# Scan kernel on one core: B tables loaded for eight steps at a time, gate loads in 256 KB pieces, next layer's weights later

## The chip, the cores and the metric

One core of a Trainium2 chip runs the whole program. The metric is the device time in microseconds (us) of one execution; the time before is the median of three runs. The engines are TensorE (PE; PEld are its weight loads), VectorE (DVE), ScalarE (ACT), GpSimd (POOL) and SyncE (SP), which here computes nothing and issues nearly all DMA transfers, one after the other ("SPq" in the rows).

## What is computed

Four residual layers on x of shape (64 sequences, 64 positions, 256 channels): two of attention, then two of a selective state space model. The change lies in the last two. Cut to what matters, for D_INNER = 512 and D_STATE = 16:

```python
xr, gate = split(x @ W_in.T); xc = silu(conv(xr + t_emb)); xn = layernorm(xc)
Bm, Cm, dt = split(xn @ W_xproj.T, 3)
Ad = 1.0 + tanh(dt @ W_dt.T + b_dt) * 0.01 * A
Bd = Bm * minimum(norm(xn), 1.0)
def step(h, inputs):                       # h: (64 sequences, 16, 512)
    ad, bd, xt, ct = inputs
    h = clip(h * ad[:, :, None] + bd[:, :, None] * xt[:, None, :], -10.0, 10.0)
    return h, einsum('bd,bdh->bh', ct, h)
y = scan(step) + D * xn                    # 64 positions, one after the other
x = x + (y * silu(gate)) @ W_out.T
```

## The kernel before

The 64 sequences are 8 groups of 8 (G = 8). Each of the two scan layers (l = 0, 1) has a front part (projections, convolution, norm, per group), a scan, and a post part (gate and output projection, per group). The scan works on four groups at once (QW = 4), so a layer has two passes of 64 steps (PASSES = 2). The state q is 128 partitions (8 sequences by 16 states) by 4 by 512, float32.

A step is a loop over three engines. PE forms the outer products B x in PSUM (`inputs`, line 1520: five matmuls with 96 rows of contraction). ACT (line 1068) and POOL (line 626) multiply the old state by the decay into R. DVE adds R to PSUM and clips in three custom instructions (line 2064). PE then forms y from the new state (`y_of`, line 1533), ACT copies it out every four steps. PSUM is not doubled for the inputs: `inputs` of step n starts when DVE has finished the first instruction of step n-1, and no earlier.

The 96 rows are 3 parts of x (bfloat16 pieces of a float32 number) by 8 sequences by 4, where the fourth is a row of zeros; B has 3 such parts as well. Partition 4r+i holds x row r and B part i. The x rows and the B tables come from DRAM, where the front part has put them (`xpart_d`, `bdiag_d`), two steps a load: `load_x(ps, k)` brings steps 2k and 2k+1 into slot k % 4 of both `Uw` (B) and `xq` (x), in three transfers of 48 KB for B (24 rows of 2 KB, line 411) and three of 192 KB for x (24 rows of 8 KB, line 415). All six raise the same semaphore `xq_in[k % 4]`, on which PE waits before an even step. The zero rows of `Uw` are set once by a memset on POOL (line 577).

SP's program is written out by hand. In each pass there are eight rounds `c2` of eight steps; a round has four turns `s8`. Each turn waits until PE has done the inputs of step 8 c2 + 2 s8 + 1 (`x_done_with`, semaphore `pe_w`), which frees one slot, and then loads steps 6 to 7 further on (`load_x(ps, 4*c2 + s8 + 4)`). Behind certain turns other work is queued, in program order:

- `store_y` in turns 0 and 2: y of four steps, 256 KB;
- in pass 0: `store_parts` (three transfers of 512 KB), `store_decay`, `store_b` (six small ones) and `store_x` of the last two groups, and in round 6 `load_tables(1)` (eight transfers of 32 KB);
- in pass 1: `load_gate(0)` behind round 1 and `load_gate(1)` behind round 2 (each two transfers of 1 MB: `xnp` and `sgp`), `load_front(1)` behind round 3 (the next layer's weights, six transfers, some 1.3 MB, layer 0 only), `load_y(0)` and `load_y(1)` behind round 4 (four transfers of 512 KB), `load_y(2)` and `load_y(3)` in round 7.

The end of a scan starts the post part, which needs the gates (semaphores `po_in`), y and Wo.

Of the kernel before, what the change touches and what calls it, by code (L numbers as in the profile page):

```python
# [10 lines left out]
P = 128  # L11
GB = P // N
# [20 lines left out]
ROW = QW * GB * N  # L33
DIAG = PARTS * S * ROW
SSM_LOADS = 6
# [8 lines left out]
def cond_resid_kernel(nc, xT, condT, attw, win, wconv, chan, wxp, wdt, dtv, wout, dskip,  # L44
# [19 lines left out]
    with es:  # L64
# [77 lines left out]

        Uw = sb("Uw", [P, XB, XT, QW, GB, N], bf16, where=ssm)
        sb("By", [P, 2, CH, QW, STRIP], bf16, where=ssm)
# [107 lines left out]
        pad_r = sem("pads_set")  # L252
        one_in = [sem("still_rows0"), sem("still_rows1")]
        zero_r, zero_in = sem("zeros_set"), sem("diagonal_zeroed")
        bt_mm, pd_r = sem("bturn_mm"), sem("decayed_odd_ready")
# [19 lines left out]
        PICK = 4 * 16  # L275
        XQ = 2 * PARTS * 16
        PW = QW + 1
# [35 lines left out]
        def _(sp):  # L313
# [25 lines left out]
            sp.wait_ge(x_done, LAYERS * G + 1)  # L339
            sp.wait_ge(set_r, 2)  # L340
            for l in range(LAYERS):
# [23 lines left out]
                def store_b(it, ps, w):  # L365
                    sp.wait_ge(tv_s, it * 4 + 4 + TV0)
                    alone(sp)
                    for b in range(2):
                        rows = bdiag_d[ps].rearrange("(j b r) -> j b r", b=2, r=DIAG + N)[:, b, 0:DIAG]
                        rows = rows.rearrange("j (i t w c n) -> i w c t j n", i=PARTS, t=S, w=QW, c=GB)  # L370
                        for i in range(PARTS):
                            sp.dma_start(rows[i, ds(w, 1), 0].rearrange("a t j n -> (a t) j n"),
                                         tvp[b * S:(b + 1) * S, i, :].rearrange("p (j r) -> p j r", r=LANE)[:, :, 0:N]).then_inc(tv_st, 16)
# [22 lines left out]
                def load_tables(ps):  # L396
                    Cc, At = pass_tables[ps]
                    q0 = ps * QW
                    for dst, src in ((Cc, cc_d), (At, a_d)):
                        for g in range(QW):  # L400
                            sp.dma_start(dst[:, g, :], src[q0 + g, :, 0:N, :]).then_inc(tab_in[ps], 16)

                def still_rows(b):
                    half_x = xq[:, b * (XB // 2):(b + 1) * (XB // 2), :, :, :].rearrange("p k g t c -> p (k g t c)")
                    for i in range(PARTS, SPREAD):
                        sp.dma_start(half_x[i:XROWS:SPREAD, :], still_d).then_inc(one_in[b], 16)

                def load_x(ps, k):
                    rows = bdiag_d[ps, 0:GB * DIAG].rearrange("(b i f) -> i b f", i=PARTS, f=S * ROW)
                    for i in range(PARTS):  # L410
                        sp.dma_start(Uw[i:XROWS:SPREAD, k % XB, :, :, :, :].rearrange("p t w b n -> p (t w b n)"),
                                     rows[i, :, k * (XT * ROW):(k + 1) * (XT * ROW)].unsqueeze(0)
                                     .broadcast_to([PARTS, GB, XT * ROW])).then_inc(xq_in[k % XB], 16)
                    for i in range(PARTS):
                        sp.dma_start(xq[i:XROWS:SPREAD, k % XB, :, :, :].rearrange("p t g c -> p (t g c)"),
                                     xpart_d[ps, :, :, k * XT:(k + 1) * XT, :, :].rearrange("j b t g c -> (j b) (t g c)")).then_inc(xq_in[k % XB], 16)
# [5 lines left out]
                def load_y(g):  # L422
                    for b2 in range(2):
                        sp.dma_start(y_tile(g)[b2 * S:(b2 + 1) * S, :, :],
                                     y_d[:, g].rearrange("k (t j b) c -> b k t j c", t=CH, b=2)[b2]).then_inc(yl_in[g % YB], 16)

                def load_gate(g):
# [27 lines left out]
                for k in range(XB // 2):  # L455
                    load_x(0, k)
                store_decay(l * G + G - 2, G - 2)
                sp.wait_ge(zc_r, l * (G * DC) + G * DC)
# [6 lines left out]
                for ps in range(PASSES):  # L465
# [5 lines left out]
                    for c2 in range(CHUNKS // 2):  # L471
                        for s8 in range(4):
# [3 lines left out]
                            if c2 + 1 < CHUNKS // 2:  # L476
                                load_x(ps, 4 * c2 + s8 + XB)
                            elif ps + 1 < PASSES:
                                load_x(ps + 1, s8)
                            elif s8 < 2:  # L480
                                alone(sp)
                                load_y(2 + s8)
                            if s8 == 0 and (c2 or ps):
                                store_y(ps - (c2 == 0), (2 * c2 - 1) % CHUNKS)
                            if s8 == 2:
                                store_y(ps, 2 * c2)
                            if ps == 0 and (c2, s8) == (0, 1):
                                store_parts(l * G + G - 2, 1, QW - 2)
# [15 lines left out]
                        if ps + 1 == PASSES and c2 == 0:  # L504
                            sp.wait_ge(sg_st, l * (16 * G) + 16 * G + 16)
                            sp.wait_ge(xf_st, l * (16 * G) + 16 * G + 16)
                            alone(sp)
                        if ps + 1 == PASSES and c2 in (1, 2):
                            load_gate(c2 - 1)
                        if ps + 1 == PASSES and c2 == 3 and l + 1 < LAYERS:  # L510
                            load_front(l + 1)
# [26 lines left out]
        def _(pl):  # L538
# [37 lines left out]
            pl.memset(Wy[:, :, :, :], 0.0).then_inc(set_r, 1)  # L576
            pl.memset(words(Uw), 0.0).then_inc(set_r, 1)
            pl.wait_ge(set_r, 2)
            alone(pl)
# [507 lines left out]
        def _(pe):  # L1087
# [253 lines left out]
            for l in range(LAYERS):  # L1341
# [168 lines left out]
                alone(pe)  # L1510
                def inputs(pi, c2, s8, first=False):
                    n = c2 * 8 + s8
                    hb = s8 // XT % XB
                    if s8 % XT == 0:
                        pe.wait_ge(xq_in[hb], (pi * (HALVES // XB) + c2 + s8 // 8) * XQ + XQ)
                    if first and s8 in (0, 4):
                        pe.wait_ge(one_in[s8 // 4], (l + 1) * (16 * (SPREAD - PARTS)))
                    for w, begin, end, bank, unit in ((0, 0, DI, 0, 1), (1, 0, DI // 2, 1, 1), (1, DI // 2, DI, 2, 2), (2, 0, DI, 3, 2), (3, 0, DI, 5, 3)):
                        pe.wait_ge(dv_q, pi * (UN * S) + n * UN + unit)
                        pe.matmul(PS[:, bank, begin:end], Uw[0:XROWS, hb, s8 % XT, w, :, :].rearrange("p b n -> p (b n)"),  # L1520
                                  xq[0:XROWS, hb, s8 % XT, w, begin:end], start=True, stop=True).then_inc(pe_w, 1)
# [14 lines left out]

                inputs(l * PASSES, 0, 0, True)
                for ps in range(PASSES):
                    pi = l * PASSES + ps
                    plain = TAIL if ps == 0 else 1  # L1540
                    for c2 in range(plain):
                        for s8 in range(8):
                            if ps == 0:
                                last_group(c2 * 8 + s8)
                            inputs(pi, c2, s8 + 1, ps == 0 and c2 == 0)
                            y_of(pi, c2, s8)
                    with pe.Fori(plain, CHUNKS // 2 - 1) as c2:
                        for s8 in range(8):
                            inputs(pi, c2, s8 + 1)
                            y_of(pi, c2, s8)  # L1550
                    for s8 in range(8):
# [39 lines left out]
        def _(v):  # L1591
# [292 lines left out]
            for l in range(LAYERS):  # L1884
# [196 lines left out]
                def gated(g):  # L2081
                    it, u = l * G + g, g % 2
                    v.wait_ge(po_in[u], (l * (G // 2) + g // 2) * 32 + 32)
                    if it:
# [88 lines left out]
```

## Time and profile before

| what | value |
|---|---|
| runs | 1834.01 us median of 3 (1826.44 to 1843.92) |
| the profiled execution | 1831.48 us, of which the span of the records is 1829.7 us |
| PE / DVE / ACT / POOL busy | 90% / 85% / 66% / 32% of the span |
| scan of layer 0 | 743.7 to 1107.7 us |
| scan of layer 1 | 1385.5 to 1745.5 us |
| DMA queue of SP | 242.57 MB, 40.6% of 16 DMA engines' span |
| xq loads, Uw loads | 384 of 192 KB, 384 of 48 KB |

Times in the profile are counted from the start of the span. A group row gives busy time and the idle time just before it with what ended it. For SP a row is the time in which it issues transfers; when they land is not in it. With two busy engines coupled by a step, the question for the scan is not who is busiest but what DVE, the engine that carries the state, waits for.

### The profile page before, as it was taken

To read this page: it belongs to the slowest core of one execution; us is meant where nothing else is said; L and a number is where in the kernel's file an instruction comes from. 1 tells how busy PE (TensorE), PEld (TensorE's weight loads), DVE (VectorE), ACT (ScalarE), POOL (GpSimd) and SP (SyncE) were. 2 spreads that over 40 slices of the span, in tenths; PEclk is the share of its full clock that TensorE was granted. 3 is DMA by queue.
4 is the path that set the end of the run, shared out by engine and by line. 5 is a ranking of instruction groups with operands and counts; after the bars stand their busy time and mean duration, and the time that the engine had idled before them with its cause. 6 is when DMAs were issued, how large, how long until landed. Compare 5 with 4: busy or idle time off the path is not lost. (4 is left out here: it accounts for less than half of the span.)

```text
span 1829.7 us, 42381 instructions
## 1 busy us (share of the span) xinstructions
PE 1640.9 (90%) x14036; PEld 714.1 (39%) x14036; DVE 1561.6 (85%) x2132; ACT 1212.6 (66%) x2017; POOL 586.8 (32%) x822
## 2 busy tenths in 40 slices
PE   7999999999999999788797879999997887978898
PEld 3555555555554555222121214445552221211144
DVE  5899999999887999889797877679998997978865
ACT  5646555555647999788777771079997887878710
POOL 0223232322321112455454540011224554545400
PEclk9999999999999999899898989999998998999899
DMA  4000003000002454555556667524545555566687
GB/s 159 2 1 0 1 2 108 2 1 0 1 1 93 160 171 169 158 176 187 160 181 227 213 203 243 177 84 168 171 163 161 180 187 162 179 219 210 197 238 261
DMA packets 123040, 245.87 MB, mean 134 GB/s; under 512 B 50000, under 2 KB 75856, under 8 KB 104912
## 3 DMA queue, kind: packets, MB, share of 16 engines
q1 hardware_dynamic: 122496, 242.57, 40.6%
q10 hardware_dynamic: 432, 1.84, 0.3%
q8 instruction: 67, 1.10, 0.2%
q14 instruction: 45, 0.37, 0.1%
HBM read 158.25 MB, written 86.11 MB: 134 GB/s over the span
## 5 line engine op out<-in xcount | busy, mean ns | idle before, releaser
L2064 DVE CUSTOM_DVE_ANT_0 q<-R,PS 128x768 f32<-128x768 f32 x756 | 597.9, 857 | 99.1 <-PE PS L1520 87.3
L1068 ACT ACTIVATE R<-q,Ast 128x512 f32<-128x512 f32 x756 | 508.9, 715 | 123.2 <-DVE q L2064 82.5
L1520 PE MATMUL PS<-xq,Uw 96*128 96x512 bf16 (+1 forms) x1280 | 342.1, 360 | 110.7 <-DMA xq<-xpart_d 65.9
L626 POOL TENSOR_TENSOR R<-q,Ast 128x256 f32<-128x256 f32 x504 | 308.5, 612 | 362.1 <-DVE q L2064 307.4
L1533 PE MATMUL PS<-q,Wy 128*32 128x512 f32 x2048 | 289.7, 632 | 3.4 <-ACT ys L1055 2.7
L1520 PEld LDWEIGHTS PS<-xq,Uw 96*128 96x128 bf16 x1280 | 93.7, 100 | 479.4 <-DVE q L2064 348.7
L1189 PE MATMUL PS<-X,Win 128*128 (+1 forms) x456 | 213.7, 606 | 0.1
L1090 PE MATMUL PS<-xn,Wl 128*128 128x512 f32 x384 | 188.0, 614 | 0.7 <-DVE xn L1646 0.7
L1764 DVE SCALAR_TENSOR_TENSOR acc<-xp,Wc,acc 128x512 f32<-128x512 f32 x192 | 134.5, 748 | 2.6
L557 POOL TENSOR_TENSOR ex<-ex,rs 128x1024 f32<-128x1024 f32 x32 | 76.8, 2400 | 164.2 <-DVE rs L1669 164.2
L1189 PEld LDWEIGHTS PS<-X,Win 128*128 128x128 f32 x456 | 82.5, 191 | 92.4 <-issue 91.6
L1573 PE MATMUL PS<-yg,Wo 128*128 128x512 f32 x256 | 113.5, 597 | 0.0
L550 POOL TENSOR_TENSOR vsc<-vTd,vs_t 128x1024 f32<-128x1024 f32 x16 | 41.6, 2602 | 216.1 <-ACT vTd L767 216.1
L791 ACT ACTIVATE acc<-xp,Ch,Wc 128x512 f32<-128x512 f32 x64 | 51.9, 815 | 76.0 <-DVE xp L1760 75.8
L775 ACT ACTIVATE pT<-PS 128x512 f32<-128x512 f32 x128 | 69.3, 594 | 41.9 <-PE PS L1167 41.9
L767 ACT ACTIVATE vTd<-PS 128x1024 f32<-128x1024 f32 x32 | 32.8, 1024 | 86.4 <-PE PS L1090 86.4
L1090 PEld LDWEIGHTS PS<-xn,Wl 128*128 128x128 f32 x384 | 66.2, 191 | 56.2 <-issue 51.8
L1656 DVE TENSOR_REDUCE mx<-PS 128x32 f32<-128x2048 f32 x32 | 73.1, 2284 | 15.1 <-PE PS L1151 14.9
L2088 DVE SCALAR_TENSOR_TENSOR yf<-xnp,Dsk,PS 128x512 f32<-128x512 f32 x64 | 43.5, 742 | 44.6 <-DMA sgp<-sg_d 38.3
L1666 DVE TENSOR_REDUCE sm<-ex 128x32 f32<-128x2048 f32 x32 | 73.0, 2281 | 7.7 <-ACT ex L779 7.7
L1167 PE MATMUL PS<-ident,ex 128*128 128x128 f32 x512 | 69.3, 277 | 7.6 <-DVE ex L1673 5.7
L1533 PEld LDWEIGHTS PS<-q,Wy 128*32 128x32 f32 x2048 | 43.9, 110 | 81.5 <-issue 73.7
(160 smaller groups left out, 2438.2 us busy)
## 6 DMA issues: line engine op xcount, KB each, us to landing
xq<-xpart_d SPq DMA_DIRECT2D x384, 192.0 KB
Uw<-bdiag_d SPq DMA_DIRECT2D x384, 48.0 KB
sg_d<-sg SPq DMA_DIRECT2D x16, 1024.0 KB, 5.5
xn_d<-z SPq DMA_DIRECT2D x16, 1024.0 KB, 4.0
y_d<-ys SPq DMA_DIRECT2D x64, 256.0 KB, 4.3
xnp<-xn_d SPq DMA_DIRECT2D x16, 1024.0 KB, 9.1
sgp<-sg_d SPq DMA_DIRECT2D x16, 1024.0 KB, 13.5
xpart_d<-xh SPq DMA_DIRECT2D x16, 512.0 KB, 3.0
```

The source lines that it names most:

```text
L557: pl.tensor_tensor(late_half(ex, r), late_half(ex, r), rs[:, r, :].rearrange("p (j e) -> p j e", j=4)[:, :, 4:8] .unsqueeze(3).broadcast_t ...
L626: pl.tensor_tensor(R[:, 1, cols], q[:, (t + 1) % 2, 1, cols], Ast[:, h, 1, t:t + 1].broadcast_to([P, DI // 2]), ALU.mult).then_inc(pd_r, 1)
L1068: act.activation(R[:, w, :], q[:, (t + 1) % 2, w, :], ACT.Copy, scale=Ast[:, h, w, t:t + 1]).then_inc(ac_r, 1)
L1090: mm = pe.matmul(PS[:, bank, :], Wl[l][:, w, c, m * P:(m + 1) * P], rhs[:, c, :], start=(c == 0), stop=(c == HC - 1))
L1189: mm = pe.matmul(PS[:, m % DC, :], Win[:, c, m * P:(m + 1) * P], X[:, ds(g, 1), c, :].rearrange("p a t -> p (a t)"), start=(c == 0), stop= ...
L1520: pe.matmul(PS[:, bank, begin:end], Uw[0:XROWS, hb, s8 % XT, w, :, :].rearrange("p b n -> p (b n)"), xq[0:XROWS, hb, s8 % XT, w, begin:end ...
L1533: mm = pe.matmul(PS[32 * w:32 * w + 32, 4, :], Wy[:, h, w, t * 32:(t + 1) * 32], q[:, s8 % 2, w, :], start=(t == 0), stop=(t == CH - 1), s ...
L1573: mm = pe.matmul(PS[:, 4 + 2 * (g % 2) + m, :], Wo[:, c, m * P:(m + 1) * P], yg[:, g % 2, c, :], start=(c == 0), stop=(c == DC - 1))
L1656: v.tensor_reduce(mx[:, r, :], PS[:, 0:4, :].rearrange("p j (e k) -> p (j e) k", k=S), AX.X, ALU.max).then_inc(max_r, 1)
L1666: v.tensor_reduce(sm[:, r, :], ex[:, r, :, :].rearrange("p j (e k) -> p (j e) k", k=S), AX.X, ALU.add).then_inc(sum_r, 1)
L1764: v.scalar_tensor_tensor(out=tiled(acc[:, m, :]), in0=xp[:, m, :, j:j + S], scalar=Wc[:, m, j:j + 1], in1=tiled(acc[:, m, :]), op0=ALU.mul ...
L2064: v._custom_dve(bass.dve_ops.TENSOR_ADD_SAT, out=state, in0=R[:, :, :].rearrange("p w c -> p (w c)")[:, begin:end], in1=fed, s0=CLIP, s1=- ...
```

## The change

- The B tables get a layout in DRAM with four parts instead of three, the fourth zero (`DIAG` grows by a third, and the zeroing of `bdiag_d` during attention from 12 to 16 transfers of 256 KB), so that 32 rows of eight steps (8 KB each) are one transfer.
- `Uw` holds two buffers of eight steps. `load_b(ps, c2)` fills one in three transfers of 256 KB, on a semaphore of its own (`u_in`). PE waits for it before the first step of each round. In a round it is issued once, in turn 3, for the round after the next.
- `load_x` issues only its three x transfers; `XQ` halves.
- At the start of the scan the order on SP is x for steps 0 to 3, then B of rounds 0 and 1, and later x for steps 4 to 7.
- `load_gate(0)` and `load_gate(1)` are split: `load_piece` brings 256 KB of `xnp` and 256 KB of `sgp` behind each x load of rounds 1 and 2 of the last pass. The later gates are loaded as before.
- `load_front(l + 1)` moves from behind round 3 to behind round 5.
- The memset of `Uw` on POOL goes, and with it one count of `set_r`.
- PE's loop over rounds has 16 steps in its body instead of 8, since the buffer of B alternates.

```diff
-DIAG = PARTS * S * ROW
+DIAG = 4 * S * ROW
+UB = 2 * 4
-        Uw = sb("Uw", [P, XB, XT, QW, GB, N], bf16, where=ssm)
+        Uw = sb("Uw", [P, 2, UB, QW, GB, N], bf16, where=ssm)
-        XQ = 2 * PARTS * 16
+        XQ = PARTS * 16
+                def load_b(ps, c2):
+                    rows = bdiag_d[ps, 0:GB * DIAG].rearrange("(r f) -> r f", f=S * ROW)
+                    for j in range(PARTS):
+                        sp.dma_start(Uw[SPREAD * GB * j:SPREAD * GB * (j + 1), c2 % 2, :, :, :, :].rearrange("p t w b n -> p (t w b n)"),
+                                     rows[:, c2 * (UB * ROW):(c2 + 1) * (UB * ROW)]).then_inc(u_in[c2 % 2], 16)
+
                 def load_x(ps, k):
-                    rows = bdiag_d[ps, 0:GB * DIAG].rearrange("(b i f) -> i b f", i=PARTS, f=S * ROW)
-                    for i in range(PARTS):
-                        sp.dma_start(Uw[i:XROWS:SPREAD, k % XB, :, :, :, :].rearrange("p t w b n -> p (t w b n)"),
-                                     rows[i, :, k * (XT * ROW):(k + 1) * (XT * ROW)].unsqueeze(0)
-                                     .broadcast_to([PARTS, GB, XT * ROW])).then_inc(xq_in[k % XB], 16)
+                def load_piece(g, m):
+                    for dst, src in ((xnp, xn_d), (sgp, sg_d)):
+                        sp.dma_start(dst[:, g % 2, m, :], src[g, :, m, :]).then_inc(po_in[g % 2], 16)
                 for k in range(XB // 2):
                     load_x(0, k)
+                load_b(0, 0)
+                load_b(0, 1)
+                            if s8 == 3 and (c2 + 2 < CHUNKS // 2 or ps + 1 < PASSES):
+                                load_b((ps + (c2 + 2) // (CHUNKS // 2)), (c2 + 2) % (CHUNKS // 2))
+                            if ps + 1 == PASSES and c2 in (1, 2):
+                                load_piece(c2 - 1, s8)
-                        if ps + 1 == PASSES and c2 in (1, 2):
-                            load_gate(c2 - 1)
-                        if ps + 1 == PASSES and c2 == 3 and l + 1 < LAYERS:
+                        if ps + 1 == PASSES and c2 == 5 and l + 1 < LAYERS:
                             load_front(l + 1)
-            pl.memset(words(Uw), 0.0).then_inc(set_r, 1)
-                def inputs(pi, c2, s8, first=False):
+                def inputs(pi, k, s8, c=None, first=False):
+                    c2 = k if c is None else c * 2 + k
+                    u, twos = (k + s8 // 8) % 2, (k + s8 // 8) // 2 + (0 if c is None else c)
+                    if s8 % 8 == 0:
+                        pe.wait_ge(u_in[u], (twos + pi * (CHUNKS // 4)) * (PARTS * 16) + PARTS * 16)
-                    with pe.Fori(plain, CHUNKS // 2 - 1) as c2:
-                        for s8 in range(8):
-                            inputs(pi, c2, s8 + 1)
-                            y_of(pi, c2, s8)
+                    with pe.Fori(0, (CHUNKS // 2 - 1 - plain) // 2) as c:
+                        for k in (plain, plain + 1):
+                            for s8 in range(8):
+                                inputs(pi, k, s8 + 1, c)
+                                y_of(pi, c * 2 + k, s8)
```

SP at the start of a scan, before. The rows name destination and source of the transfers, their shape and their number; `still_d` is zeros, `cc_d` and `a_d` are stores of group 6, `tvp` its B.

```order
L406 DMA xq<-still_d 24x8192
L411 DMA Uw<-bdiag_d 24x1x1024 x3
L415 DMA xq<-xpart_d 24x4096 x3
L411 DMA Uw<-bdiag_d 24x1x1024 x3
L415 DMA xq<-xpart_d 24x4096 x3
L356 DMA cc_d<-Cn 4x32x64 x2
L356 DMA a_d<-am 4x32x64 x2
L406 DMA xq<-still_d 24x8192
```

The same place in the changed kernel:

```order
L407 DMA xq<-still_d 24x8192
L417 DMA xq<-xpart_d 24x4096 x6
L412 DMA Uw<-bdiag_d 32x4096 x6
L358 DMA cc_d<-Cn 4x32x64 x2
L358 DMA a_d<-am 4x32x64 x2
L407 DMA xq<-still_d 24x8192
```

Step 0 now needs B of round 0, which is issued behind x of steps 0 to 3; the number of transfers ahead of the stores stays twelve.

SP in the second pass of layer 0, before: turns 2 and 3 of round 1, the first gate loads, turn 0 of round 2.

```order
L411 DMA Uw<-bdiag_d 24x1x1024 x3
L415 DMA xq<-xpart_d 24x4096 x3
L420 DMA y_d<-ys 128x512
L411 DMA Uw<-bdiag_d 24x1x1024 x3
L415 DMA xq<-xpart_d 24x4096 x3
L428 DMA xnp<-xn_d 128x2048
L429 DMA sgp<-sg_d 128x2048
L411 DMA Uw<-bdiag_d 24x1x1024 x3
L415 DMA xq<-xpart_d 24x4096 x3
L420 DMA y_d<-ys 128x512
```

The same turns in the changed kernel:

```order
L417 DMA xq<-xpart_d 24x4096 x3
L422 DMA y_d<-ys 128x512
L431 DMA xnp<-xn_d 128x512
L431 DMA sgp<-sg_d 128x512
L417 DMA xq<-xpart_d 24x4096 x3
L412 DMA Uw<-bdiag_d 32x4096 x3
L431 DMA xnp<-xn_d 128x512
L431 DMA sgp<-sg_d 128x512
L417 DMA xq<-xpart_d 24x4096 x3
L422 DMA y_d<-ys 128x512
```

The six transfers of a turn have become three, the B load comes once a round, and the gates come in two quarter-size transfers a turn instead of two whole ones between two turns.

## Rows read from the trace of the kernel before

**Rows 1.** Waits of DVE, whole program: engine, line, awaited, us in total, times, longest.

```profile
DVE q L2064 <- PE PS L1520: 87.3, 47, 7.9
DVE q L2064 <- ACT R L1068: 6.4, 10, 1.2
```

**Rows 2.** Waits of PE, whole program, same columns.

```profile
PE PS L1520 <- DMA xq<-xpart_d: 65.9, 25, 7.8
```

**Rows 3.** Windows: the four passes; length, busy us, PE clock, DMA share, GB/s.

```profile
743.70:930.90 187.20, 156.88 (x977) 40.76 (x975) 160.97 (x217) 144.44 (x228) 90.00 (x165) 0.93 0.54 174
930.90:1107.70 176.80, 149.55 (x833) 33.77 (x832) 151.18 (x193) 135.39 (x205) 84.61 (x155) 0.92 0.66 208
1385.50:1570.00 184.50, 154.85 (x977) 40.38 (x975) 160.97 (x216) 144.48 (x228) 89.98 (x165) 0.94 0.54 175
1570.00:1745.50 175.50, 148.65 (x834) 33.26 (x832) 151.24 (x193) 135.48 (x205) 84.69 (x155) 0.94 0.65 204
```

**Rows 4.** Timeline of DVE, layer 0: start, length, instructions, idle before and releaser.

```profile
875.10 2.42 DVE L2064 CUSTOM_DVE_ANT_0 q<-R,PS 128x768 f32<-128x768 f32 x3 [4.32 <-PE PS L1520]
...
996.27 2.42 DVE L2064 CUSTOM_DVE_ANT_0 q<-R,PS 128x768 f32<-128x768 f32 x3 [6.89 <-PE PS L1520]
...
1019.62 2.42 DVE L2064 CUSTOM_DVE_ANT_0 q<-R,PS 128x768 f32<-128x768 f32 x3 [2.84 <-PE PS L1520]
...
1041.13 14.20 DVE L2064 CUSTOM_DVE_ANT_0 q<-R,PS 128x768 f32<-128x768 f32 x18 [0.72 <-PE PS L1520]
...
1068.52 2.42 DVE L2064 CUSTOM_DVE_ANT_0 q<-R,PS 128x768 f32<-128x768 f32 x3 [7.91 <-PE PS L1520]
1072.21 35.53 DVE L2064 CUSTOM_DVE_ANT_0 q<-R,PS 128x768 f32<-128x768 f32 x45 [1.27 <-PE PS L1520]
```

**Rows 5.** Timeline of SP, second pass, round 0: start and length of the issuing.

```profile
940.43 2.24 SPq L411 DMA_DIRECT2D Uw<-bdiag_d  x3
942.72 2.30 SPq L415 DMA_DIRECT2D xq<-xpart_d  x3
945.06 0.52 SPq L420 DMA_DIRECT2D y_d<-ys  x1
```

**Rows 6.** Waits of SP in the window 743.7 to 930.9.

```profile
SPq L411 <- PE PS L1520: 10.4, 19, 1.2
```

**Rows 7.** Timeline of SP and PE around the first load_y of layer 0.

```profile
1048.19 1.28 SPq L424 DMA_DIRECT2D y_space<-y_d  x2
1049.52 1.26 SPq L424 DMA_DIRECT2D spare_y<-y_d  x2
1050.82 2.32 SPq L411 DMA_DIRECT2D Uw<-bdiag_d  x3
1053.19 2.30 SPq L415 DMA_DIRECT2D xq<-xpart_d  x3
...
1067.52 1.88 PE L1520 MATMUL PS<-xq,Uw 96*128 96x512 bf16 x5 [7.78 <-DMA xq<-xpart_d]
```

**Rows 8.** Windows of 2 us in pass 1; last three columns clock, DMA share, GB/s.

```profile
984.00:986.00 2.00, 2.00 (x14) 0.60 (x15) 1.36 (x2) 0.97 (x2) 0.25 (x2) 1.00 1.00 360
990.00:992.00 2.00, 0.00 (x0) 0.00 (x0) 0.00 (x0) 0.15 (x1) 0.00 (x0) 0.72 0.73 232
1056.00:1058.00 2.00, 1.91 (x14) 0.38 (x12) 2.00 (x3) 1.09 (x3) 0.74 (x2) 1.00 1.07 218
```

**Rows 9.** Timeline of SP and PE at the first step of layer 0.

```profile
736.02 2.31 SPq L415 DMA_DIRECT2D xq<-xpart_d  x3
...
742.83 2.45 PE L1520 MATMUL PS<-xq,Uw 96*128 96x512 bf16 x6
```

**Rows 10.** Timeline of DVE: waits for PE where no load is late.

```profile
769.95 2.41 DVE L2064 CUSTOM_DVE_ANT_0 q<-R,PS 128x768 f32<-128x768 f32 x3 [0.46 <-PE PS L1520]
...
933.78 6.47 DVE L2064 CUSTOM_DVE_ANT_0 q<-R,PS 128x768 f32<-128x768 f32 x8 [0.49 <-PE PS L1520]
...
1454.31 2.42 DVE L2064 CUSTOM_DVE_ANT_0 q<-R,PS 128x768 f32<-128x768 f32 x3 [0.62 <-PE PS L1520]
```

## What the change should do to the time

> **What bounds the kernel now.** I read the waits of DVE first, since DVE carries the state through the scan. It waited 87.3 us for PE's inputs, 47 times, and only 6.4 us for ACT [rows 1]. PE's own waits name the cause: 65.9 us, 25 times, for the load of x [rows 2]; 87.3 is more because PE restarts slowly behind each such wait. The windows of the four passes give the frame: 724.0 us in all, DVE busy 160.97 + 151.18 + 160.97 + 151.24 = 624.4, so 99.6 us idle [rows 3]. The timeline of DVE says where: a run of 45 instructions, 15 steps, takes 35.53 us, 2.37 us a step, without a gap; the big gaps are single, 4.32 us in pass 0 and 6.89, 2.84, 0.72 and 7.91 us in pass 1, each followed by one of some 1.2 us [rows 4].
>
> Why is x late? The timeline of SP shows 2.24 us to issue three B transfers and 2.30 us for three x transfers, 0.76 us each, and 0.52 us for a y store [rows 5]. With the 0.05 us between groups a turn costs 4.63 us, a store 0.57, and a round of eight steps 4 x 4.63 + 2 x 0.57 = 19.7 us. DVE needs 8 x 2.37 = 19.0 us for it. SP is slower than DVE before anything else is queued on it: in 187 us of pass 0 it waited 10.4 us for PE to free slots [rows 6]. Whatever stands in front of a load (parts, tables, gates, front weights, y) then makes SP late, and the lateness is never won back until DVE stalls.
>
> The worst case in full: step 39 began at 1026.21 + 5 x 2.37 = 1038.1 us and step 41 at 1041.13 + 2.37 = 1043.5 [rows 4], which frees the slot of step 48. SP issued that load from 1050.8 on, 7.3 us late, behind y loads issued from 1048.19; it landed at 1067.52, where PE had waited 7.78 us [rows 7].
>
> **The change part by part.** *B tables.* Per round 12 transfers of 0.75 us become three. Their issue is not in the trace; the nearest rows are the x transfers with rows of 8 KB too, 0.77 us [rows 5], and I take that: a round costs SP 12 x 0.77 + 3 x 0.77 + 2 x 0.57 = 12.7 us of 19.0. From below nothing bounds it but zero; from above, 1.5 us a transfer would still give 14.9. SP then waits for PE at each turn, and a load has its full lead: from the end of the inputs of step 2k+1, which is the start of that step on DVE, to the inputs of step 2k+8, six steps and 0.9 us later, 15.1 us. An x load alone needs 2.3 us to issue and little more to land: at the first step its last issue began near 737.6 and PE used it at 742.83 without waiting, so 5.3 us at most [rows 9]. Slack 15.1 - 2.3 - 5.3 = 7.5 us or more, where there was none. The other work on SP's queue is three to eight transfers in a round, at 0.77 us each no more than 6.2 us, and a round leaves 19.0 - 12.7 = 6.3.
>
> What this can take back is the DVE waits that a load causes. I subtract from 87.3 us those that stay: ten gaps behind PE's work for the last group, the first 0.46 and the last 0.62, 6.1 us together, and 0.49 us at step 1 of each second pass [rows 10], in all 7.1. **Removable: 80.2 us.**
>
> *Gates in pieces.* 8 turns of a layer carry 512 KB more. The full rate was 360 GB/s with the 1 MB transfers under way, 232 where x loads were left alone, and 218 with rows of 2 KB, as the pieces have [rows 8]. A turn then moves 576 KB of x (2.5 us), 192 KB of B at 360 (0.5), 512 KB of gates at 218 (2.3) and 128 KB of y at 218 (0.6): 5.95 us against 4.74. If nothing overlaps, 8 x 1.21 = 9.7 us pile up against a slack of 7.5: at most 2.2 us a layer. If x and gates overlap, as the 360 GB/s suggest, nothing. I take 0. SP's own time for the pieces, 8 x 0.64 as for the y loads [rows 7] = 5.1 us a round, brings a round to 17.8 us, below 19.0.
>
> *The first load_y* is not split, so it is the one burst left. Before, 19.3 us passed from its first issue to the landing of the load behind it [rows 7]. Now it is issued when step 39 has begun, behind x (2.3) and B (2.3), at +5 us, and the load behind it is needed at step 48's inputs, +19.9. With the old 19.3 us it lands at +24.3, a stall of 4.4 us and 1.3 behind it; with bytes alone (0.77 of B, 2.1 of y, 0.58 of x, 0.26 stored, at 360 to 218 GB/s, 10.3 to 17 us) it lands at +15.3 to +22. Range 0 to 5.7 us a layer; I take 2.0, nearer to the bytes, since the old case had two B sets and a second x load in flight: **-4.0 us**.
>
> For those bytes the Trainium skill has a rule, page "DMA: Bandwidth & Descriptors", section "Why a DMA increments its semaphore by 16 and not by 1": a transfer runs on the largest number of engines up to 16 that divides the slowest dimension of both sides. By it the old B transfers (a broadcast dimension of 3) ran on 3 engines, x (24 rows) on 12, and the new B (32 rows) on 16; the trace agrees as far as the DMA share of 0.73 with only x and B loads left goes [rows 8], and no row shows single engines. By an estimate from that page the most loaded engines then carry 60 KB a turn instead of 96, and the term here would be 0 and not 4: 1753 us.
>
> *The start.* B of round 0 is the third group issued, its last issue one group of 2.3 us later than that of x for step 0 was, so it lands 0 to 2.3 us after PE asks at 742.83 [rows 9]. I take 1.0 a layer: **-2.0 us**.
>
> *At nothing:* four more zeroing transfers and the memset lie in attention, where SP idles; the front weights now follow round 5 with 15 steps of the pass left, and the post part of layer 0 needs them last; B's loads have a lead of over eight steps. PE's loop executes the same matmuls per step in a longer body; before, the 15 steps at 2.37 us ran out of the loop into straight code without a gap [rows 4]. DVE, ACT and POOL keep their work; the idle ACT waits I leave in.
>
> **Sum.** 80.2 - 4.0 - 2.0 = 74.2 us off the profiled execution's 1831.48: 1757 us. The median of the runs, 1834.01, lies 2.5 us above it, inside their spread of 17, and I add nothing.
>
> **Rivals.**
> *A. The bursts cost, not SP's lateness.* For it: 7.3 us of lateness stand beside 19.3 us of transfer [rows 7], and the pieces bring the same bytes with shorter rows. Against: SP issued without a pause where no burst was near [rows 5], and the 4.32 us of pass 0 [rows 4] fell behind a smaller burst, the 1.5 MB of the part stores. Then the y stall stays whole, 9.2 us in layer 0 and about as much in layer 1, and half of the others, 5.5, 8.2 and 4.1 us with their second gaps: 18.4 + 17.8 = 36 us remain, 1831.5 - 80.2 + 36 = **1788 us**, with the start's 2 us well inside the roundness of this.
>
> *B. The change does not do what it says: issuing is not the limit.* The Trainium skill says on the same page, "Issuing engines are not separate DMA queues", that the time to initiate is "usually small relative to the DMA itself". As a mechanism of this kernel: x moves 576 KB a turn at 232 GB/s, 2.5 us, plus y and B; were that what fills the 4.7 us of a turn, only the B bytes would matter, and they grow by a third. Then the stalls stay but for 10 us at the gates: **1822 us**. Against it: 4.54 us of issuing in a turn of 4.74 [rows 5], which is not small; the page's sentence would leave this rival the likeliest.
>
> *C. Slower: B late each round.* PE now waits for B before 28 rounds whose B is loaded during the scan. If B came late, all of those would stop. Break-even is 74.2 / 28 = 2.7 us each; 1% slower, 92 / 28 = 3.3 us: **1850 us**. B's issue ends 5 us after step 8c+7 begins and is needed 9 x 2.37 - 1.5 = 19.8 us after it, 14.8 us later; to be 3.3 late it would need 18 us from its last issue. Behind the y burst a load took 12.8 us at worst [rows 7]. Little speaks for it.
>
> **How the numbers follow.** The forecast 0.73, its own range 1746 to 1771: all 80.2 and a part of ACT's 6.4 gone below; y stall in full, gates 2.2 and start 2.3 in each layer above (7.4 + 4.4 + 2.6 = 14 us). A 0.16, B 0.05, C 0.03, and 0.03 for better than 1746. The range to be held 8 times in 10 reaches from 1744 to 1788: it takes in the forecast and the better half of A. About 1% is what a measurement of this kernel can tell from no change, so faster means below 1816: the forecast, A and the better case, 0.92; same 0.05; slower 0.03.
>
> **What would show it.** Right: DVE's wait for PE falls from 87.3 to some 13 us; PE's wait for x nearly goes; SP waits for PE some 6 us in a plain round; steps 24, 32 and 44 without a gap; a gap of 0 to 5.7 us at step 48. Wrong: gaps before steps 33 to 40 (gate pieces), waits for Uw at multiples of eight (C), or SP still issuing without a pause (B transfers dearer than 0.77 us). If DVE's instructions or ACT's get longer with more DMA traffic beside them, the floor of 2.37 us a step falls as a basis.

## Result: 1770 us, 3.3% faster

| | us | runs |
|---|---|---|
| before | 1831.35 median (1826.44 to 1843.92) | 4 |
| changed kernel | 1770.45 median (1761.81 to 1774.35) | 4 |
| ratio | 0.9665, 95% interval 0.9629 to 0.9701 | |
| changed kernel, profiled execution | 1761.81, span 1760.0 | |
| forecast | 1757, range 1744 to 1788 | |

Waits in the changed kernel, whole program: engine, line, awaited, us in total, times, longest. Lines 2078 and 2075 are DVE's steps (2075 is the first of a pass), 1533 PE's inputs, 417 the x loads on SP.

```profile
DVE q L2078 <- PE PS L1533: 13.0, 16, 1.7
DVE q L2075 <- PE PS L1533: 12.8, 2, 6.7
DVE q L2078 <- ACT R L1077: 7.5, 8, 1.2
PE PS L1533 <- DMA Uw<-bdiag_d: 10.3, 2, 5.4
PE PS L1533 <- DMA xq<-xpart_d: 8.0, 7, 2.0
SPq L417 <- PE PS L1533: 177.5, 109, 3.7
```

DVE's wait for PE in the steps fell from 87.3 to 13.0 us [rows 1], PE's wait for x from 65.9 to 8.0 us [rows 2]. SP waits 177.5 us for free slots. In the kernel before it was a quarter of that:

```profile
SPq L411 <- PE PS L1520: 43.6, 70, 2.4
```

A wait that was not there has appeared: 10.3 us for `Uw`, twice, before the first step of each scan.

The four passes as windows, with the columns of [rows 3]:

```profile
748.30:916.40 168.10, 153.91 (x978) 38.00 (x975) 160.23 (x217) 144.54 (x228) 89.90 (x165) 0.97 0.70 206
916.40:1071.30 154.90, 143.90 (x835) 31.76 (x834) 150.43 (x193) 135.27 (x205) 84.51 (x155) 1.00 0.87 236
1351.80:1520.80 169.00, 155.31 (x977) 38.26 (x975) 160.22 (x216) 144.52 (x228) 89.91 (x165) 0.96 0.70 204
1520.80:1676.30 155.50, 143.97 (x835) 31.87 (x836) 150.62 (x193) 135.40 (x205) 84.58 (x155) 1.00 0.84 227
```

Together 647.5 us against 724.0, DVE busy 621.5 of them (624.4 before), so 26.0 us idle against 99.6. DVE works as long as before and waits less. The granted clock of PE in the second pass is 1.00 in both layers, instead of 0.92 and 0.94. Before, it was down to 0.72 in a stretch in which PE stood idle [rows 8]; idle times of 7 us are gone from that pass. The start of the two scans gave back 12.8 - 2.4 = 10.4 us of DVE's waits (2.4 is what DVE waited there before); PE waited 5.4 and 4.9 us for B. The windows begin behind those waits and so do not hold them. The passes gave 724.0 - 647.5 = 76.5 us, the starts took 10.4: 66.1 of the 69.7 us by which the span is shorter are thereby found. The other 3.6 are spread over the parts outside the scans.

SP in the second pass of the changed kernel, start and length of the issuing:

```profile
933.82 2.27 SPq L417 DMA_DIRECT2D xq<-xpart_d  x3
936.13 1.44 SPq L412 DMA_DIRECT2D Uw<-bdiag_d  x3
938.47 2.29 SPq L417 DMA_DIRECT2D xq<-xpart_d  x3
940.80 0.51 SPq L422 DMA_DIRECT2D y_d<-ys  x1
```

An x transfer costs SP 0.76 us as before [rows 5], a B transfer with 32 rows only 0.48. Between them SP pauses.

### The profile page after: what moved, and what is told of

Read it like the earlier page. It is cut to its first block and busy times, and to the rows that moved or that the text cites. A ratio compares the mean times of both kernels' runs of the same rounds, so it can differ in the third digit from the quotient of the medians.

```text
span 1760.0 us, 42112 instructions
## 1 busy us (share of the span) xinstructions
PE 1627.5 (92%) x14036; PEld 705.4 (40%) x14036; DVE 1559.0 (89%) x2132; ACT 1212.5 (69%) x2017; POOL 584.7 (33%) x821
## 3 DMA queue, kind: packets, MB, share of 16 engines
q10 hardware_dynamic: 432, 1.84, 0.3%
## 5 line engine op out<-in xcount | busy, mean ns | idle before, releaser
L1546 PE MATMUL PS<-q,Wy 128*32 128x512 f32 x2048 | 280.9, 613 | 2.6 <-ACT ys L1064 1.9
L1533 PEld LDWEIGHTS PS<-xq,Uw 96*128 96x128 bf16 x1280 | 85.7, 97 | 437.7 <-DVE q L2078 374.6
L2102 DVE SCALAR_TENSOR_TENSOR yf<-xnp,Dsk,PS 128x512 f32<-128x512 f32 x64 | 43.6, 743 | 42.3 <-DMA sgp<-sg_d 36.0
L611 POOL CAST middle<-remain 128x128 bf16<-128x128 f32 x14 | 4.1, 293 | 218.7 <-DVE remain L1912 218.7
```

The lines of the kernel that those rows point to most:

```text
L1533: pe.matmul(PS[:, bank, begin:end], Uw[0:XROWS, u, s8 % 8, w, :, :].rearrange("p b n -> p (b n)"), xq[0:XROWS, hb, s8 % XT, w, begin:end], ...
L1546: mm = pe.matmul(PS[32 * w:32 * w + 32, 4, :], Wy[:, h, w, t * 32:(t + 1) * 32], q[:, s8 % 2, w, :], start=(t == 0), stop=(t == CH - 1), s ...
```

## Experiments

Each ran beside the kernel before on its chip; ratios are to that. Edits are shown against the changed kernel where nothing else is said; arrays, counts and waits that only follow from them are left out. The theories: SP's issuing is too slow for DVE (*lateness*); the few DMA engines on which B and x run are the limit (*few engines*); the large transfers hold the loads up (*bursts*).

### B alone

```diff
-                            if ps + 1 == PASSES and c2 in (1, 2):
-                                load_piece(c2 - 1, s8)
+                        if ps + 1 == PASSES and c2 in (1, 2):
+                            load_gate(c2 - 1)
-                        if ps + 1 == PASSES and c2 == 5 and l + 1 < LAYERS:
+                        if ps + 1 == PASSES and c2 == 3 and l + 1 < LAYERS:
```

> The changed kernel with only the B tables changed: the first gates come in whole transfers of 1 MB behind rounds 1 and 2, and the front weights behind round 3, as before the change. Theory of SP's lateness: a load has 15 us of lead, so the bursts are mostly hidden; 0 to 4 us of stalls a layer, 1770 to 1778 us. Theory of the bursts: the stalls at steps 24 and 32 of the second passes come back, 8.4 + 4.3 us in each layer: about 1795 us.

Measured: 1766.85 us (1761.01 to 1774.52), ratio 0.9675 (0.9630 to 0.9721). The B tables bring the whole gain. Timeline of DVE in the second pass of layer 0 of this kernel:

```profile
917.92 111.15 DVE L2078 CUSTOM_DVE_ANT_0 q<-R,PS 128x768 f32<-128x768 f32 x141 [0.49 <-PE PS L1533]
1037.91 2.42 DVE L2078 CUSTOM_DVE_ANT_0 q<-R,PS 128x768 f32<-128x768 f32 x3 [8.84 <-PE PS L1533]
1041.59 35.47 DVE L2078 CUSTOM_DVE_ANT_0 q<-R,PS 128x768 f32<-128x768 f32 x45 [1.27 <-PE PS L1533]
```

141 instructions, steps 1 to 47, run without one gap past the whole gate loads and the front weights; at step 48, behind the y loads, 8.84 us remain. So the bursts theory falls for the gates; behind y a stall is left in this layer. Here the front weights had gone by shortly before y. In layer 1, which loads none, the gap at step 48 was 0.45 us.

### The gates in pieces, alone

```diff
-                        if ps + 1 == PASSES and c2 in (1, 2):
-                            load_gate(c2 - 1)
+                            if ps + 1 == PASSES and c2 in (1, 2):
+                                load_piece(c2 - 1, s8)
```

This is the kernel before with these lines (and DVE's counts for `po_in`).

> The kernel before with only the first two gates loaded in pieces of 256 KB behind the x loads. Theory of SP's lateness and of the few engines alike: neither is relieved, SP gets 12 more transfers to issue in these two rounds, the stalls move but stay: 1820 to 1838 us. Theory of the bursts: the stalls at steps 24 and 32 go, some 12 us a layer: about 1805 us.

Measured: 1826.47 us (1823.61 to 1835.75), ratio 0.9999 (0.9975 to 1.0023). No effect. DVE waited 86.0 us for PE, in 54 places instead of 47: the stalls were only shared out.

### SP kept busy

```diff
+                            if c2 + 1 < CHUNKS // 2 or ps + 1 < PASSES:
+                                for n in range(2 if s8 == 0 else 3):
+                                    sp.dma_start(idle_d[(pi * 4 * (CHUNKS // 2) + 4 * c2 + s8) * 3 + n], still_d[:, 0:32]).then_inc(idle_in, 16)
```

> The changed kernel with 11 tiny copies a round added on SP's queue (24 rows of 64 bytes from the array of zeros into unused DRAM): by 0.77 us each, 8.5 us of issuing, so that a round costs SP about 19.8 us again, as before the change, with no bytes to speak of. Theory of SP's lateness: the stalls come back, 1815 to 1835 us. Theory that the transfers' own load on few DMA engines was the limit: 1770 to 1778 us.

Measured: 1836.27 us (1834.35 to 1846.11), ratio 1.0048 (1.0029 to 1.0067). Its waits:

```profile
DVE q L2084 <- PE PS L1539: 89.2, 49, 10.8
PE PS L1539 <- DMA xq<-xpart_d: 72.3, 26, 10.7
SPq L419 <- PE PS L1539: 46.8, 70, 1.5
```

The copies carry 1.5 KB each. Issuing alone takes the whole gain back, and the waits look like those before the change: 89.2 for 87.3 us [rows 1], 72.3 for 65.9 [rows 2], and 46.8 us of SP for free slots where the kernel before had 43.6. The transfers themselves were not slower: from the first to the last event that a load of x raised on its semaphore passed 4.5 us in the median, 5.6 in the changed kernel. SP's lateness is shown as a cause.

### Three DMA engines kept busy

```diff
+                            if c2 + 1 < CHUNKS // 2 or ps + 1 < PASSES:
+                                sp.dma_start(idle_d[pi * 4 * (CHUNKS // 2) + 4 * c2 + s8, :, 0:GB * 3072].rearrange("j (b c) -> j b c", b=GB),
+                                             still_d[:, 0:3072].rearrange("(j b) c -> j b c", b=GB)).then_inc(idle_in, 16)
```

> The changed kernel with one copy a turn added, 3 by 8 rows of 6 KB (144 KB, as many bytes as the old B loads of a turn) from the array of zeros into unused DRAM, its slowest dimension 3. SP: 4 x 0.77 = 3.1 us more a round, 14.7 of 19.0 us. Theory of SP's lateness: 1765 to 1780 us. Theory of the few engines (if such a copy runs on 3 of 16, these carry 108 KB a turn, above the 96 of the kernel before): stalls of x come back, 1820 us or more.

Measured: 1859.01 us (1856.53 to 1862.20), ratio 1.0161 (1.0130 to 1.0193), with SP waiting 123.5 us for free slots. Slower than the kernel before. Two questions follow: was it the bytes as such or their spread, and would less have done?

The same 144 KB as 16 rows of 9 KB:

```diff
-                                sp.dma_start(idle_d[pi * 4 * (CHUNKS // 2) + 4 * c2 + s8, :, 0:GB * 3072].rearrange("j (b c) -> j b c", b=GB),
-                                             still_d[:, 0:3072].rearrange("(j b) c -> j b c", b=GB)).then_inc(idle_in, 16)
+                                sp.dma_start(idle_d[pi * 4 * (CHUNKS // 2) + 4 * c2 + s8, :, 0:4608], still_d[0:16, 0:4608]).then_inc(idle_in, 16)
```

> The changed kernel with one copy a turn of 144 KB as 16 rows of 9 KB, from and to the same arrays as in the run with 3 by 8 rows of 6 KB (1859 us). If the number of engines made that run slow, this one, 9 KB an engine, stays within 1% of the changed kernel: 1765 to 1782 us. If the bytes, the array of zeros or the writes to DRAM made it slow, 1840 us or more.

Measured: 1773.85 us (1768.58 to 1780.35), ratio 0.9690 (0.9665 to 0.9715), within the interval of the changed kernel's. And 3 by 8 rows of 4.5 KB, 108 KB, with which three engines would carry 96 KB a turn, as much as in the kernel before:

```diff
-                                sp.dma_start(idle_d[pi * 4 * (CHUNKS // 2) + 4 * c2 + s8, :, 0:GB * 3072].rearrange("j (b c) -> j b c", b=GB),
-                                             still_d[:, 0:3072].rearrange("(j b) c -> j b c", b=GB)).then_inc(idle_in, 16)
+                                sp.dma_start(idle_d[pi * 4 * (CHUNKS // 2) + 4 * c2 + s8, :, 0:GB * 2304].rearrange("j (b c) -> j b c", b=GB),
+                                             still_d[:, 0:2304].rearrange("(j b) c -> j b c", b=GB)).then_inc(idle_in, 16)
```

> The changed kernel with one copy a turn of 3 by 8 rows of 4.5 KB (108 KB) from the array of zeros into unused DRAM. If it runs on 3 DMA engines, these carry 60 + 36 = 96 KB a turn, as much as in the kernel before, while SP has 11.6 + 2.8 = 14.4 of 19.0 us a round to issue. Theory that the few engines were a limit of their own in the kernel before: 1815 to 1845 us, PE waiting for x while SP waits for PE. Theory that only SP's issuing was the limit at that load, and the 108 KB of the earlier run went too far: 1770 to 1785 us.

Measured: 1818.97 us (1811.97 to 1822.73), ratio 0.9930 (0.9904 to 0.9955). Its waits:

```profile
DVE q L2084 <- PE PS L1539: 68.3, 41, 9.1
PE PS L1539 <- DMA xq<-xpart_d: 54.0, 21, 9.0
SPq L419 <- PE PS L1539: 117.7, 92, 5.8
```

SP waits 117.7 us for free slots, so it is not late, and yet PE waits 54.0 us for x. With 108 KB and a slowest dimension of 3 the time is within 0.7% of the kernel before; with 144 KB in 16 it is that of the changed kernel. The shape of a transfer decides, not its bytes.

By the Trainium skill, page "DMA: Bandwidth & Descriptors", section "Why a DMA increments its semaphore by 16 and not by 1", a transfer runs on the largest number of engines up to 16 that divides the slowest dimension of both sides. The traces agree in the number of events with which a transfer raises its semaphore by 16: 4 for a copy of 3 by 8 rows and for an old B transfer, 13 for x, 16 for a new B transfer and for the copy of 16 rows. That is 3, 12 and 16, and one event more where there are fewer than 16. (The two old transfers are counted together: a load of B and x has 51 events, 3 by 4 and 3 by 13.)

The times of these events show where PE's wait comes from. A load of x has 39 of them: three that come while SP issues, and twelve for each of the three transfers as they land. Take the load that SP began to issue at 942.88 us in the run with 3 by 8 rows of 4.5 KB. Its first 30 events, 27 of them landings, had come by 948.89. Then there was none until 956.51, and the last came at 958.68. Nine is three for each transfer. From the 30th event to the last passed 5.4 us in the median of the 128 loads; in the changed kernel it was 1.1 us, with the 16 rows 1.0, with SP kept busy 0.4. An event does not name its engine; that the nine are those of the three engines with the copy on them is inferred from their number.

How much of this was in the kernel before? Of the 51 events there, the last 18 are all that three engines would raise for B and x together. From the 33rd to the last passed 1.8 us in the median, so these copies weighed more than the old B loads did. Of PE's 65.9 us of waiting for x, at most 39.7 fell behind the 33rd event. In the run with the copies 47.8 of 54.0 fell behind the 30th, and with SP kept busy, where B has its new shape, 21.4 of 72.3. At the worst stall before, step 48 [rows 7], the 33rd event came at 1063.40 and the last at 1067.38: 4.0 of the 7.8 us.

So either limit alone can cost this scan 49 to 66 us (1819 and 1836 against 1770). The issuing brought back alone gives the time of the kernel before, 1836 against 1831, with the new B transfers in place: by these runs their shape without the smaller number of issues would have brought nothing. What the old shape alone would have cost was not run; by the events it is less than the 49 us of the copies.

### The start of the scan

```diff
+                load_b(0, 0)
                 for k in range(XB // 2):
                     load_x(0, k)
-                load_b(0, 0)
-                load_b(0, 1)
...
                 for k in range(XB // 2, XB):
                     load_x(0, k)
+                load_b(0, 1)
```

> The changed kernel with one order altered at the start of each scan: B of round 0 is issued ahead of x of steps 0 to 3, and B of round 1 behind x of steps 4 to 7. Changed kernel: PE waits 5.4 us a layer for the first B. If B was late because of its place in the queue, PE's wait before the first step falls to 0 to 2 us in each layer and the time by 8 to 11 us, to about 1761. If the start is short of transfer rate (zero rows, x and B together), x becomes the late one instead and at most 3 us are gained.

Measured: 1760.53 us (1746.76 to 1764.46), ratio 0.9602 (0.9553 to 0.9652). DVE's wait before its first steps fell from 12.8 to 5.4 us, of which 2.4 are PE's own time: 3.0 are left of 10.4. The interval of the ratio overlaps that of the changed kernel, 0.9629 to 0.9701, so the gain is read from the waits. (The waits with B first that the next expectation quotes, 0.6 to 1.5 us, were set down too low: they were 1.0 and 2.0.) Is it the place behind x, or B of round 1 beside it?

```diff
                 load_b(0, 0)
-                load_b(0, 1)
...
                     load_x(0, k)
+                load_b(0, 1)
```

> The changed kernel with B of round 1 issued behind x of steps 4 to 7, B of round 0 left behind x of steps 0 to 3; one look, for PE's wait before the first step (5.4 and 4.9 us in the two layers of the changed kernel, 0.6 to 1.5 with B of round 0 first). If the place of B of round 0 behind x makes it late, the wait stays at 4 us or more. If the 768 KB of B of round 1, which are under way beside it, make it late, the wait falls below 2.5 us.

Measured once: 1774.89 us. PE waited 10.3 us for `Uw` in the two layers, 5.58 in layer 0: as in the changed kernel. The place behind x makes B late. That execution had a stall of 8.45 us at step 48 of the second pass, though its program is the changed kernel's there. The profile of the changed kernel shows 1.41. Why that load was late here is open.

### The y loads in halves

```diff
-                            load_y(0)
-                            load_y(1)
+                            if ps + 1 == PASSES and c2 == 5:
+                                load_y_half(s8 // 2, s8 % 2)
-                        if ps + 1 == PASSES and c2 == 5 and l + 1 < LAYERS:
+                        if ps + 1 == PASSES and c2 == 6 and l + 1 < LAYERS:
```

with B first as above.

> The changed kernel with B of round 0 first at the start, the first two y loads in four halves of 512 KB, one behind each turn of round 5 and not together behind round 4, and the front weights behind round 6. The gaps of 1 to 2 us in the second half of pass 1 go (some 3 us a layer) and so do the 3.7 us a layer of the start: 1755 us, 8 to 14 below the changed kernel. If the gaps come from the total rate (the DMA share was 0.91 there), they only move, and the time is that of the kernel with B first, 1760 us.

Measured: 1754.62 us (1751.01 to 1763.78), ratio 0.9611 (0.9577 to 0.9646), against 0.9602 with B first alone: too close to tell by the ratios. By the profile the second pass of layer 0 ran without a gap, while in layer 1 steps 30 to 33 still had gaps of 1.23, 3.54 and 1.26 us. There stand the gate pieces.

### The gate pieces on trial

Three kernels side by side on one chip. The changed kernel again:

> The changed kernel once more, beside the two below on one chip. 1762 to 1774 us as before; the spread should come from the stall at step 48 of the second pass of layer 0 (1.4 us in its first profile, 8.5 us in the run with B of round 1 later, which is alike there).

Measured: 1770.20 us (1764.98 to 1772.42), ratio 0.9672 (0.9647 to 0.9697). DVE in the second pass of layer 0, steps 24, 26, 32, 48 and 56:

```profile
973.22 4.74 DVE L2078 CUSTOM_DVE_ANT_0 q<-R,PS 128x768 f32<-128x768 f32 x6 [0.40 <-PE PS L1533]
981.10 2.42 DVE L2078 CUSTOM_DVE_ANT_0 q<-R,PS 128x768 f32<-128x768 f32 x3 [3.14 <-PE PS L1533]
...
999.91 2.42 DVE L2078 CUSTOM_DVE_ANT_0 q<-R,PS 128x768 f32<-128x768 f32 x3 [2.78 <-PE PS L1533]
...
1040.08 18.85 DVE L2078 CUSTOM_DVE_ANT_0 q<-R,PS 128x768 f32<-128x768 f32 x24 [1.48 <-PE PS L1533]
1061.49 2.42 DVE L2078 CUSTOM_DVE_ANT_0 q<-R,PS 128x768 f32<-128x768 f32 x3 [2.55 <-PE PS L1533]
```

In this execution DVE waited 27.5 us for PE in the steps, not 13.0. The first profile was of the fastest of its four runs, 1761.81; this one is of the slowest of its six, 1772.42. My guess that step 48 makes the spread did not hold here (1.48 us); the gaps at 26 and 32 do it, and one of 3.47 us at step 30 in layer 1.

The changed kernel with whole gates (`load_gate` behind rounds 1 and 2, as in the diff of B alone, front weights behind round 5):

> The changed kernel with the first two gates in whole transfers behind rounds 1 and 2. If the pieces help, the stalls at steps 24 and 32 come back, some 5 us or more: 1775 us. If a lead of 15 us hides the whole gates as well, there is no difference beyond the noise; if the pieces are what makes the gaps of 1 to 3 us at steps 30 to 32, it is 1 to 5 us faster: 1765 to 1770.

Measured: 1758.05 us (1754.24 to 1764.07), ratio 0.9612 (0.9585 to 0.9638), 12 us below the changed kernel with intervals that don't meet, and more than the 1 to 5 us expected. Its second passes:

```profile
922.13 111.13 DVE L2078 CUSTOM_DVE_ANT_0 q<-R,PS 128x768 f32<-128x768 f32 x141 [0.49 <-PE PS L1533]
1034.32 18.85 DVE L2078 CUSTOM_DVE_ANT_0 q<-R,PS 128x768 f32<-128x768 f32 x24 [1.06 <-PE PS L1533]
...
1525.70 111.16 DVE L2078 CUSTOM_DVE_ANT_0 q<-R,PS 128x768 f32<-128x768 f32 x141 [0.49 <-PE PS L1533]
```

Steps 1 to 47 in one piece in both layers. And the two findings together, with the y halves and the front weights behind round 6:

> B of round 0 first, whole gates, the first two y loads in halves over round 5, front weights behind round 6. If the pieces of the gates cost 2 to 5 us, this is the fastest version: 1748 to 1753 us. If not, it is as fast as the version with pieces, 1755 us.

Measured: **1746.57 us** (1744.57 to 1749.42), ratio 0.9551 (0.9527 to 0.9574): 24 us below the changed kernel and the fastest version of the study. Its second passes, whole:

```profile
917.71 148.99 DVE L2082 CUSTOM_DVE_ANT_0 q<-R,PS 128x768 f32<-128x768 f32 x189 [0.49 <-PE PS L1537]
...
1512.80 149.03 DVE L2082 CUSTOM_DVE_ANT_0 q<-R,PS 128x768 f32<-128x768 f32 x189 [0.49 <-PE PS L1537]
```

63 steps in 149.0 us, 2.365 us each, no gap. DVE is the bound of these passes now.

What the pieces do to the transfers can be read from one window of each kernel, at the same place in the turns of the gates of layer 0, 46.4 us behind the start of the pass (last columns DMA share and GB/s). First the changed kernel again, then the first profile of the changed kernel, then whole gates:

```profile
962.00:982.00 20.00, 15.91 (x95) 3.82 (x91) 16.40 (x22) 14.96 (x23) 9.58 (x18) 0.94 0.98 232
```

```profile
962.80:982.80 20.00, 19.20 (x116) 4.19 (x108) 19.87 (x26) 18.12 (x28) 11.53 (x22) 1.00 0.99 271
```

```profile
965.60:985.60 20.00, 19.21 (x116) 4.24 (x108) 19.87 (x26) 18.13 (x28) 11.49 (x22) 1.00 0.94 273
```

With pieces the DMA engines are full, and what they move differs from one execution to the next, 232 and 271 GB/s; with whole gates they move 273 and are busy 0.94 of the time. So the pieces leave no room, though in a good execution they move as much. The shorter rows, 2 KB instead of 8, would fit that. But the pieces also stand behind eight x loads instead of two, and the two were not separated.

## Why the prediction was right, and where it was not

- **What bounds it: right, and half of it.** SP's lateness was read from rows and the run with SP kept busy shows it. The second limit I let move only one term, by 4 us. Copies of that shape cost 49 us, and of PE's 65.9 us of waiting in the kernel before up to 39.7 may be its part. The rows showed a sign of it: the load behind the y burst landed 19.3 us after the burst began [rows 7], while the bytes alone account for 10 to 17, and I put the difference down to loads in flight. 4.0 us of it passed behind the 33rd of its 51 events.
- **80.2 us removable: right in kind.** In the steps 87.3 - 13.0 = 74.3 us went in the first profile, 87.3 - 27.5 = 59.8 in the second. My sum left 7.1 + 4.0 = 11.1 us in this row. Of the 13.0, 6.7 are the gaps behind PE's other work and at step 1 (forecast 7.1), and 6.3 are stalls by loads.
- **B at 0.77 us a transfer: too dear.** 0.48 us, so a plain round costs SP 11.7 us and not 12.7. Without effect, since SP waits anyway.
- **The start, -2.0 us: mis-sized.** It was 10.4 us. I took the landing of x at the head of the queue (5.3 us at most [rows 9]) for B, which stands behind the zero rows and two x loads. SP began to issue it at 737.46 us and PE got it at 747.49, some 8.6 us behind the last issue of that B where I had 5.3 at most. The run with B first shows the cause, the place in the queue.
- **Gates in pieces at nothing: wrong.** I bounded them at 2.2 us a layer; by the medians they cost 12 us together. The step that failed is the overlap: I took 0 because x and gates together seemed to move at 360 GB/s. A turn has 1408 KB, 1.44 MB, and the windows above show 232 and 271 GB/s with the engines full. An estimate from them: 6.2 or 5.3 us a turn against 4.74, over 8 turns 11.8 or 4.7 us too much, against a slack of 7.5. That leaves 4.3 us a layer to stall in the slow case and none in the fast one. The profiles show both: in layer 0 of the first no wait for PE at the pieces, in layer 0 of the second 8.9 us from step 24 to 33, even more than this. My case without overlap, 5.95 us a turn, was the right one to take. The Trainium skill, page "DMA: Bandwidth & Descriptors", section "Measured (HBM→SBUF, 128 partitions, SWDGE, issued from GpSimd)", advises transfers of at least 1 MiB; the runs agree in direction, 1758 us with 1 MB against 1770 with 256 KB, though on another queue.
- **The y burst, -4.0 us: about right.** 1.41 and 1.10 us at step 48 of the two layers in the first profile, 1.48 and 1.84 + 0.83 in the second, but 8.45 once.
- **The front weights, at nothing: a small term missed.** Behind round 5 they are followed by a gap at step 56 of layer 0, 1.51 us in the first profile and 2.55 + 0.79 in the second; layer 1, which loads none, has no gap there. What their old place costs is not shown. Whole gates with the front weights behind round 3 gave 0.9675, behind round 5 0.9612 (two separate comparisons, their intervals just overlap), and the stalls at step 48 were 8.84 and 1.06 us. But 8.45 us came once with the front weights behind round 5 too.
- **Errors that met, and some luck.** Against the forecast of 74.2 us off the span, the first profile has 69.7. The steps gave 74.3 where I had 76.2, and the starts took 10.4 where I had 2.0. Two things that I had not counted made up for most of this: 3.6 us outside the scans and 624.4 - 621.5 = 2.9 us of DVE's busy time; waits for ACT took 1.1. The median is 9 us above this profile, which is of the fastest run; in the second profile, 11 us slower, the waits at the gate pieces are 13.9 us instead of 2.3. That the time came within 13 us of the forecast is partly luck.
- **The rivals.** A (bursts) fell with B alone at 1767 us. I had priced it too low as well: my reading of pass 0 left out its largest gap, at step 58, and so the like of it in layer 1, 5.05 us. With these A is some 7 us dearer. B (issuing is not the limit) fell with SP kept busy. C (B late each round) did not occur: PE waited for `Uw` only at the two starts. The gap at step 58, before:

```profile
915.41 2.42 DVE L2064 CUSTOM_DVE_ANT_0 q<-R,PS 128x768 f32<-128x768 f32 x3 [5.78 <-PE PS L1520]
```

## What to carry to other kernels

When an engine waits for loads, add up the issuing time of a period on the queue and set it against the period: 24 transfers at 0.76 us and two stores filled this scan's round. Look also at the slowest dimension of a transfer: copies with one of 3 held up the x loads beside them, copies of more bytes with 16 rows did not. The events that a transfer raises on its semaphore show in how many parts it runs and whether some of them are late. A transfer that is put first in time but not first in need is late, so order the start of a phase by first use. Once loads have a real lead, splitting large transfers into small ones can cost more than it saves: measure the whole ones again.

## What the runs showed of the hardware

- A transfer of 24 rows costs SP 0.72 to 0.77 us to issue whether a row has 8 KB, 2 KB or 64 bytes (the tiny copies took 2.17 us for three). One of 32, 64 or 128 rows costs 0.42 to 0.65 us. The copy of 3 by 8 rows took 0.70 us, that of 16 rows 0.53.
- A transfer raised its semaphore in 4 events with a slowest dimension of 3, in 13 with 24 rows, in 16 with 16 or 32 rows.
- A copy of 108 KB with a slowest dimension of 3, once in a turn of two steps, slowed a stream of other loads by 49 us in the program. One of 144 KB with 16 rows slowed it by 3 us, within the noise.
- With SP's issuing back at its old length the shape of the B transfers made no difference: 1836 us with the new shape, 1831 with the old one.
